# A fused transformer block: feed-forward weight pieces fetched from the sync queue, one split per step of cross-attention, and batch 1's statistics in two steps

## The reference

```python
h = _layernorm(x, ln1_g, ln1_b)
x = _attention(h, h, sa_wq, sa_wk, sa_wv, sa_wo, sa_bo) + x
h = _layernorm(x, ln2_g, ln2_b)
x = _attention(h, cond_emb, ca_wq, ca_wk, ca_wv, ca_wo, ca_bo) + x
h = _layernorm(x, ln3_g, ln3_b)
p = h @ ff_w1 + ff_b1
a, gate = (p[..., :D_FF], p[..., D_FF:])
h = a * jax.nn.gelu(gate, approximate=False) @ ff_w2 + ff_b2
return h + x
```

## Time and profile before

| | |
|---|---|
| median of 3 runs | 1070.79 us (1067.57, 1070.79, 1071.01) |
| the profiled execution | 1067.25 us, of it span 1065.5 us |
| PE busy | 1025.8 us, 96% of the span |
| DVE busy | 831.1 us, 78% |
| ACT busy | 626.1 us, 59% |
| POOL busy | 307.7 us, 29% |
| granted TensorE clock | 0.997 of full speed |

### The profile page before, as it was taken

One profiled execution on the slowest core, in us unless ns is written; L12 is line 12 of the kernel. 1 busy time (PEld: TensorE's weight loads), 2 busy tenths in 40 slices (PEclk: granted clock), 3 DMA queues, 4 the chain that ended last, 5 costly groups with the idle time before them and its releaser, 6 DMA issues.

```text
span 1065.5 us, 28582 instructions
## 1 busy us (share of the span) xinstructions
PE 1025.8 (96%) x12258; PEld 834.5 (78%) x12258; DVE 831.1 (78%) x971; ACT 626.1 (59%) x1127; POOL 307.7 (29%) x280
## 2 busy tenths in 40 slices
PE   7999999999998999999999999998998998999998
PEld 5777777777776788777777777776687988888887
DVE  4778888889889888888888889898868898645433
ACT  4756666666666666666665666675755644443322
POOL 5102322323232123423223223221314357701000
PEclk9999999999999999999999999999999999999999
DMA  9896676577666866675785667597210001100000
GB/s 187 235 207 158 136 154 150 126 141 148 130 138 123 193 128 132 125 167 118 145 181 116 128 136 153 116 224 150 46 61 21 1 21 50 31 1 20 20 2 39
DMA packets 178366, 121.37 MB, mean 114 GB/s; under 512 B 142656, under 2 KB 158528, under 8 KB 173760
## 3 DMA queue, kind: packets, MB, share of 16 engines
q1 hardware_dynamic: 177280, 116.40, 50.7%
q0 software_dynamic: 960, 3.15, 1.0%
HBM read 56.60 MB, written 12.58 MB: 65 GB/s over the span
## 4 chain that ended last, share of the span: by engine, by line
PE 80%; DVE 7%; ACT 5%; issue 4%; POOL 2%; DMA 1%; SPq 0%; DVEq 0%; ACTq 0%; POOLq 0%
PE W L627 21%; PE SC L602 18%; PE W L639 10%; PE SC L691 8%; PE W L575 7%; PE W L701 4%; PE W L585 4%; PE W L867 3%; ACT OTF L955 3%; PE SC L679 2%; DVE nmax L1169 2%; DVE PR L1174 2%; POOL PR L515 1%; PE W L854 1%; ACT PR L947 1%
## 5 line engine op out<-in xcount | busy, mean ns | idle before, releaser
L947 ACT ACTIVATE PR<-SC,nmax 128x1024 f32<-128x1024 f32 x256 | 285.8, 1116 | 224.6 <-DVE nmax L1169 224.1
L1169 DVE TENSOR_REDUCE nmax<-SC 128x1 f32<-128x1024 f32 x256 | 307.9, 1203 | 107.8 <-PE SC L602 107.6
L1174 DVE STREAM_TRANSPOSE PR<-PR 128x1024 f32<-128x1024 f32 x256 | 314.9, 1230 | 0.1
L464 POOL TENSOR_TENSOR X<-f_raw,X 128x512 f32<-128x512 f32 x128 | 165.0, 1290 | 497.1 <-ACT f_raw L966 497.0
L602 PE MATMUL SC<-QKS 128*128 128x512 f32 x1024 | 297.2, 416 | 5.3 <-ACT PR L947 4.8
L627 PE MATMUL W<-PR,V 32*64 32x256 f32 x8192 | 239.7, 379 | 3.5 <-DMA V<-scratch_v 2.3
L602 PEld LDWEIGHTS SC<-QKS 128*128 128x128 f32 x1024 | 184.2, 188 | 65.3 <-issue 23.5
L627 PEld LDWEIGHTS W<-PR,V 32*64 32x64 f32 x8192 | 187.1, 132 | 49.9 <-issue 22.6
L639 PE MATMUL W<-wo,OTF 128*128 128x256 f32 x512 | 134.4, 385 | 8.2 <-ACT OTF L955 7.2
L639 PEld LDWEIGHTS W<-wo,OTF 128*128 128x128 f32 x512 | 93.9, 189 | 37.3 <-ACT OTF L955 21.1
L966 ACT ACTIVATE f_raw<-W,rden 128x256 f32<-128x256 f32 x256 | 106.5, 473 | 0.1
(11 more groups left out here) (130 smaller groups left out, 1410.9 us busy)
## 6 DMA issues: line engine op xcount, KB each, us to landing
QKS<-QKT SPq DMA_DIRECT2D x64, 512.0 KB, 6.3
V<-scratch_v SPq DMA_DIRECT2D x128, 256.0 KB, 5.0
QKS<-QKT SPq DMA_DIRECT2D x128, 128.0 KB, 4.9
scratch_v<-VST SPq DMA_DIRECT2D x32, 256.0 KB, 4.7
wo<-in_L_xattn_sa_wo_dram SPq DMA_DIRECT2D x64, 64.0 KB, 3.0
f_raw<-in_L_xattn_ff_w_dram POOLq DMA_DIRECT2D x12, 256.0 KB, 3.3
X<-in_x_dram SPq DMA_DIRECT2D x4, 512.0 KB, 4.9
w_raw<-in_L_xattn_sa_wk_dram SPq DMA_DIRECT2D x16, 128.0 KB, 3.0
```

The costliest lines, as they stand in the source:

```text
L464: nc.gpsimd.tensor_tensor(xs, f_raw[:, k % 2, :], xs, ALU.add).then_inc(p_x, 1)
L947: nc.scalar.activation(PR[:, NT * s + t, :], SC[t % 2][:, :], ACT.Exp, bias=nmax[:, t % 4:t % 4 + 1], accum_out=den[:, s, t:t + 1]).then_i ...
L1169: V.tensor_reduce(nmax[:, t % 4:t % 4 + 1], SC[t % 2][:, :], AX, ALU.max, negate=True).then_inc(d_max, 1)
L1174: V.transpose(tile, tile).then_inc(d_tr, 1)
```

## The change

Four things are changed.

1. The 12 fetches leave POOL. They stand in SP's program now, between the loading of the last value tile and the stores of the result, with the same waits: the first two for the last reads of `f_raw` by self-attention (`p_x`), each later one for the split of the piece two before it (`p_f`).
2. POOL splits one piece in each of its steps 8 to 15, and four after them; before it split 2, 2, 1, 1, 1, 1, 1, 1 and then two. The condition on `s_cs` and `s_co` still stands ahead of the first W1 piece, in step 10.
3. The pieces come in another order: W2's 0 and 1, then four of W1 (0, 4, 2, 6, which hold the columns of the first blocks), then W2's 2 and 3, then W1's 1, 5, 3, 7. PE's wait ahead of the first `ff_up` is for 6 pieces, no longer 8.
4. DVE takes the statistics of batch 1 (8 row tiles) in steps 2 and 3, four tiles in each; before it took all 8 at the end of step 2.

```diff
@@ in front of the engines' programs
+        PIECES = [("W2", 0), ("W2", 1)] + [("W1", c) for c in (0, 4, 2, 6)] + [("W2", 2), ("W2", 3)] + \
+                 [("W1", c) for c in (1, 5, 3, 7)]
@@ block.sync
             sp.wait_ge(s_pv, 8 * HS)
             sp.dma_start(VB1[:, :, :], KV_d[1, :, 1, :].rearrange("p (n c) -> p n c", c=P)).then_inc(m_vb[1], 16)
+            for n, (kind, c) in enumerate(PIECES):
+                stage = f_raw[:, n % 2, :]
+                if n < 2:
+                    sp.wait_ge(p_x, 4 * HS - 1 + n)
+                else:
+                    sp.wait_ge(p_f, n - 1)
+                if kind == "W2":
+                    sp.dma_start(stage.rearrange("p (f d) -> p f d", d=D),
+                                 ff_w2[2 * P * c:2 * P * (c + 1), :].rearrange("(f p) d -> p f d", p=P)).then_inc(m_f[n % 2], 16)
+                else:
+                    sp.dma_start(stage, ff_w1[P * (c // 4):P * (c // 4 + 1), BANK * (c % 4):BANK * (c % 4 + 1)])\
+                      .then_inc(m_f[n % 2], 16)
             for q in range(2 * B):
                 sp.wait_ge(d_fx, 2 * (q + 1))
@@ block.gpsimd
-            PIECES = [("W2", c) for c in range(4)] + [("W1", c) for c in (0, 4, 2, 6, 1, 5, 3, 7)]
-
-            def fetch(n):
-                if n >= len(PIECES):
-                    return
-                kind, c = PIECES[n]
-                stage = f_raw[:, n % 2, :]
-                if n >= 2:
-                    pool.wait_ge(p_f, n - 1)
...
-                dma.then_inc(m_f[n % 2], 16)
@@ the main loop of block.gpsimd
-            for n in range(2):
-                pool.wait_ge(p_x, 4 * HS - 1 + n)
-                fetch(n)
             for C in range(B * NT):
...
                 if C >= 8:
-                    for n in ((0, 1), (2, 3), (4,), (5,), (6,), (7,), (8,), (9,))[C - 8]:
-                        if n == 0:
-                            pool.wait_ge(s_vw, 8)
-                        if n == 4:
-                            pool.wait_ge(s_cs, NT)
-                            pool.wait_ge(s_co, NT)
-                        split_piece(n)
-                        fetch(n + 2)
-            for n in (10, 11):
+                    if C == 8:
+                        pool.wait_ge(s_vw, 8)
+                    if C == 10:
+                        pool.wait_ge(s_cs, NT)
+                        pool.wait_ge(s_co, NT)
+                    split_piece(C - 8)
+            for n in range(8, 12):
                 split_piece(n)
@@ block.tensor
                     if C == NC:
-                        pe.wait_ge(p_f, 8)
+                        pe.wait_ge(p_f, 6)
@@ block.vector
-                if C == 2:
+                if C in (2, 3):
                     dve.wait_ge(p_x, 4 * HS)
-                    ln_stats(1, range(NT))
+                    ln_stats(1, range(4 * (C - 2), 4 * (C - 2) + 4))
```

## The result

| | before | after |
|---|---|---|
| median (lowest to highest) us | 1068.74 (1065.88 to 1073.33), 8 runs | 1063.24 (1060.91 to 1065.67), 8 runs |
| profiled execution, its span us | 1067.25, 1065.5 | 1063.16, 1061.4 |

The ratio on record is 0.9942, its interval 0.992 to 0.9964: faster, by 0.58%, or 3.8 to 8.5 us (the two medians alone lie 5.5 us apart, 0.51%). The forecast was 1065.0 us in a range of 1061.5 to 1069.0. The spans differ by 4.1 us, just what the sum had given; in part that is luck, since after's cross-attention began 0.34 us later.

A forecast was written before the change was run, and what follows sets the result against it. PE was taken to set the end, its waits for POOL's `crec` multiplication being what can be won. 0.73 + 3.31 + 0.3 - 0.2 = 4.1 us saved from a mean of 1069.2 gave 1065.0 us, range 1061.5 to 1069.0.

The forecast's parts named there:

- Statistics, 0.73 us: Cross-attention tiles 2 and 3: splitting batch 1's statistics removes a 1.56 us PE wait, a new wait takes 0.83; 0.73 saved.
- Pace and queue, 3.31 us: Tiles 9 and 10: one split per step and no fetches on POOL let PE's tile 10 transposes start 3.31 us earlier.
- Tail, gain 0.3 us: After step 15: the later biases no longer hold up DVE's low part of block 0, so PE gains 0.3 us.
- Tail, loss 0.2 us: After step 15: the later biases meet DVE's low part of block 1; loss between 0 and 0.47 us, taken as 0.2.
- a sum of 4.3: Total saving in us if DVE gets in between the two biases, so that the tail loses nothing.
- The biases block DVE longer: Rival, tail: later data keep the biases in DVE's way until 936.9; 2.5 us saved, time 1066.7 us; chance 0.13.
- DVE is the real bound: Rival: second half of statistics eats the first term, `mr` still held by POOL; 2.3 us saved, 1066.9 us; chance 0.14.
- Does not bring it: Rival: PE arrives earlier but waits for ACT or DVE at the next tiles; under 1 us saved, 1068.5 us; chance 0.08.
- Slower: Rival, tail: last pieces come late, PE waits 6.6 us ahead of F = 4; time 1071.5 us; chance 0.03.
- The other signs: First `ff_up` about 4 us earlier; PE's wait about 0.8 us at tile 3, none at tiles 2 and 9.

The follow-up runs named there:

- e1: Kernel before with only the statistics of batch 1 split over steps 2 and 3; ratio 1.0007 to before, 0.81 us saved locally.
- e4: Changed kernel with all eight statistics of batch 1 back at the end of step 2; ratio 0.9947 to before, 3.69 us saved locally.
- e2: Kernel before with one split per step, the new piece order and PE waiting for 6, fetches still on POOL; ratio 0.996, 3.71 us saved locally.
- e3: Kernel before with only the 12 fetches moved to SP, old order, pace and PE wait; ratio 0.9961 to before, 3.41 us saved locally.
- e5: Changed kernel with the biases of quarters 4 and 5 in one POOL instruction; one run, 1067.29 us, 3.60 us saved locally against before.
- v1: Changed kernel with four tiles' statistics of batch 1 taken ahead of step 2, only their aggregates in it; ratio 0.9942 to before, 5.49 us saved locally.
- v2: Changed kernel with tile 1's sum and inverse and both batches' statistics moved into DVE's idle places; ratio 0.9909 to before, 6.90 us saved locally.
- e6: Changed kernel with each fetch waiting for the split of the piece just before it, one transfer in flight; ratio 1.0012 to before.

## Why the prediction was right, point by point

**Statistics, 0.73 us: right.** From tile 1's transposes to tile 3's it was 833.42 - 816.84 = 16.58 us and is 833.01 - 817.20 = 15.81: 0.77. e1 gives 0.81, e4 0.74. Of its parts, tile 2 gained 1.56 as foreseen, and tile 3 waits 0.63 with some 0.2 us unlabelled, for the 0.83 that had been worked out. ACT's square root cost nothing.

**Pace and queue, 3.31 us: right in size.** From tile 8 to tile 10 it was 887.10 - 869.80 = 17.30 us and is 883.34 - 869.45 = 13.89: 3.41. Tile 9's wait is gone, tile 10's is 0.73. `mr` took 0.17 us, where 0.26 had been estimated. What the prediction left unsaid is that the two edits are redundant: it took the bias, two splits and two fetches as one load, and e2 and e3 show that taking the pace or the fetches away is enough by itself, within 0.3 us. The size came out because the sum stopped where `crec` takes over as the bound, and did not count all that POOL is relieved of; e2's 0.68 us of idle POOL shows that bound.

**Tail, gain 0.3 us: right.** From tile 10 to the last addition it was 174.02 us and is 173.69: 0.33. Block 0's low part takes 0.68 us.

**Tail, loss 0.2 us: wrong, by its size.** It was 0. The term had two steps. The data came 3.23 and 3.35 us after their release, not 3.78, so the biases started a little earlier than thought, and still in block 1's way. That alone brings the term as it was worked out to 0: in e5, where DVE gets no turn, the low part ends at 934.95, and PE could not have used it before 934.38 + 0.81 = 935.19 (in after it is 0.81 us from the last score matmuls, at 931.10, to the down projection, at 931.91). And DVE did get its turn between the two biases: the low part took 0.94 us, not about 3.8, which the prediction had named as the sign to look for; that sign was wrong. Before's own trace held a hint that the prediction did not use: in the list by line the second bias starts at 928.3 us, just ahead of the low part's start at 928.49, so the 2.81 us were spent behind one bias and not behind two.

The rule that the prediction took from the Trainium skill ("SBUF — State Buffer", section "Who interferes with whom"), that the first to start holds the ports for its whole instruction, agrees with both cases, 0.94 us with two instructions and 3.14 in e5 with one. (That page of the Trainium skill says "for the whole instruction" of DVE's two-port modes; of a DVE instruction with two SBUF inputs it says that it contends.) The prediction's reading of the rule, a sum of 4.3, is the nearer one to 4.43. The other page of the Trainium skill ("DMA: Bandwidth & Descriptors", section "Latency and other measured facts") agrees in direction: from issue to landing the W1 pieces took 3.4 us as a median from POOL in before and 3.2 from SP after, the W2 pieces 3.2 and 2.7, so 0.2 and 0.5 us less where the two figures of the Trainium skill for the first byte, 0.6 and 1 us, differ by 0.4.

**The rivals.** *The biases block DVE longer* needed later data; they came earlier. Its condition, a low part held to the end of the biases, is e5's, and there the price came through `hT_lo`, which stood in no term. *DVE is the real bound* was half right as to what comes next (tile 10's last 0.73 us are DVE's, and v1 and v2 win by relieving DVE), but wrong as a bound of this change: e1 shows 3.25 us of wait without any stall of DVE. *Does not bring it*: excluded by an interval that ends at 0.9964. *Slower*: its condition did not come, the data were there 3.23 and 3.35 us after their release and PE did not wait ahead of F = 4; e6 made it happen. Its working priced only the wait; behind a wait of 4 us PE lost 1.55 us more to the clock, and a wait of its 6.6 us would, I infer, have cost more than 6.6.

**The other signs.** The first `ff_up` starts 115.6 us after the first scores, where it was 119.7: 4.1 us earlier, as foreseen. PE's wait at tile 3 and the missing ones at tiles 2 and 9 came too.

**The total.** 4.1 us forecast, 4.43 measured locally, 4.1 in the spans. The medians differ by 5.5 us, and both figures lie in the interval of 3.8 to 8.5. The time of 1065.0 was 1.8 us high: 0.5 since I took 1069.2 as the level of before, whose eight runs have 1068.74, and the rest is the difference between 5.5 and 4.1, which eight runs on each side leave open. The lower end of the range does not follow from its working: 1069.2 - 4.9 - 1.8 is 1062.5, and cutting the least likely ends would narrow the range, not widen it to 1061.5. The result lies above either.

## What to carry to other kernels

A wait put down to one engine has a queue behind it: ask what that engine itself would have waited for had it been on time, because that is all you can win, and every further relief of it is worth nothing (0.68 us of idle POOL in e2, 1.57 in after, the same wait of PE). Of two edits that relieve the same engine, count the gain once. When a stall moves along an engine, look at what is queued behind the stalled instruction, not only at the instruction (e5), and when medians scatter more than the terms, measure between two fixed points of the program.

## What the runs showed of the hardware

- The granted clock of TensorE was at 0.50 from PE's first matmul on after an idle time of 3.88 us in e6, and stayed there for about 3 us, which cost 1.55 us on top of the wait. In before, an idle time of 3.23 us ahead of tile 10 left it at 1.00 over the stretch around it. So the longer of these two waits had a second price, and the shorter had none.
- DVE gets its turn between two POOL instructions that stand back to back: 0.94 us for its low part in after, against 3.14 in e5 behind one instruction for the same work. The two biases took 5.21 us then, not 4.76.
- Who starts first decides who is held, here by 0.01 us: `mr` started 0.01 us behind POOL's TENSOR_TENSOR in before and took 1.32 us, and 0.01 us ahead of it in e1 and took 0.17. In after and e2 it started in the last 0.09 and 0.11 us of POOL's instruction and was not held. It works the other way too: POOL's TENSOR_TENSOR took 1.73 us and not 1.29 when it started 0.10 us behind DVE's low part.
- Pieces of 256 KB landed 3.2 us after SP's issue and 3.4 after POOL's (medians of the W1 pieces), and SP's issue took 0.33 us of a queue that had nothing else to do, where POOL paid 0.58 and a pause of 0.30.
- Self-attention, untouched by any edit, ends up to 5.7 us apart in ten profiles. In the three profiles that come to the first scores at 795 us PE is busy for 17.5 to 18.3 of the 20 us from 480 to 500, where it is 19.77 in before, and the profile shows nothing that it waited for. The cause stays open.
